# Layer 1 of a two-layer kernel: row maxima turned by DMA, projection tiles in the score banks, value pieces in halves

## What is computed

```python
Xn = (X - mu) * rsqrt(var + LN_EPS) * ln_w + ln_b
Q, K, V = split(einsum('bsd,df->bsf', Xn, W_in), 3)      # 16 heads of 16 channels
Q, K = _rope(Q), _rope(K)
scores = einsum('bhqd,bhkd->bhqk', Q, K) / sqrt(16)       # 1024 x 1024, no mask
ctx = einsum('bhqk,bhkd->bhqd', softmax(scores), V)
out = einsum('bsd,df->bsf', ctx, W_out) + X
```

## Time and profile before

| | us |
|---|---|
| median of 3 runs | 1045.62 (1043.57 to 1057.51) |
| the profiled execution | 1048.43 |
| its span, first to last instruction | 1046.6 |
| busy: PE, DVE, POOL, ACT | 924.7, 855.2, 705.1, 684.8 |

### The profile page before, as it was taken

How to read it: one execution, slowest core, us unless ns; L and a number is a source line. 1 busy time by engine, 2 the same in 40 slices (tenths; PEclk the granted TensorE clock), 3 DMA queues, 4 the chain that set the end, 5 groups by cost and what they waited for, 6 DMA issues and landing times. The chain is left out here.

```text
span 1046.6 us, 26415 instructions
## 1 busy us (share of the span) xinstructions
PE 924.7 (88%) x8703; PEld 514.1 (49%) x8703; DVE 855.2 (82%) x1760; ACT 684.8 (65%) x1779; POOL 705.1 (67%) x1034
## 2 busy tenths in 40 slices
PE   3588898998998998998998987788999999999998
PEld 2365665765666666665665665433222222323223
DVE  6797868788888888888788786578999999999871
ACT  2555655655655656565665554217999999898895
POOL 4668878788788888888888878342766765544231
PEclk9698989999999999999999998879999999999999
DMA  5655653454444543444554444243221122222101
GB/s 194 127 115 122 105 95 75 93 106 80 93 97 83 95 99 80 91 98 81 94 98 78 90 86 90 52 131 62 63 38 26 23 42 42 52 40 49 28 1 42
DMA packets 247995, 82.57 MB, mean 79 GB/s; under 512 B 222196, under 2 KB 246452, under 8 KB 247604
## 3 DMA queue, kind: packets, MB, share of 16 engines
q1 hardware_dynamic: 247428, 78.53, 37.5%
q10 hardware_dynamic: 432, 2.36, 0.6%
HBM read 18.49 MB, written 4.19 MB: 22 GB/s over the span
## 5 line engine op out<-in xcount | busy, mean ns | idle before, releaser
L1343 DVE TENSOR_REDUCE l_mxv<-l_mx 128x1 f32<-128x1024 f32 x256 | 294.9, 1214 | 26.2 <-PE l_mx L1545 25.4
L1256 ACT ACTIVATE l_prob<-l_sc 128x512 f32<-128x512 f32 x512 | 273.3, 604 | 17.6 <-PE l_sc L1553 16.5
L427 ACT ACTIVATE an<-an 128x256 f16<-128x256 f32 x128 | 53.3, 416 | 212.8 <-DVE an L601 212.8
L752 POOL TENSOR_TENSOR t<-t 128x320 f32<-128x320 f32 x128 | 110.6, 864 | 114.0 <-DVE t L648 113.9
L1545 PE MATMUL l_mx<-early 48*128 48x512 f16 x512 | 156.3, 387 | 17.7 <-DVE l_mxv L1343 14.5
L743 POOL TENSOR_TENSOR rm<-ss,half_neg 128x5 f32<-128x5 f32 x128 | 156.5, 1223 | 0.0
L1553 PE MATMUL l_sc<-early 50*128 50x512 f16 x512 | 155.7, 382 | 0.3 <-ACT l_prob L1256 0.3
L1516 PE MATMUL l_acc<-l_prob,qkv_all 128*17 128x256 f32 x2048 | 153.9, 384 | 0.0
L881 PE MATMUL qk<-early,xh 128*128 128x384 f16 x512 | 131.2, 339 | 4.4 <-issue 4.0
L934 PE MATMUL ob<-wo_hi,ats 128*128 128x256 f16 x512 | 108.4, 279 | 28.2 <-DMA ats<-an 22.7
L868 PE MATMUL pv<-v,probs 128*64 128x65 f32 x2048 | 90.4, 232 | 29.3 <-ACT probs L476 22.2
(11 more groups left out here) (191 smaller groups left out, 2069.6 us busy)
## 6 DMA issues: line engine op xcount, KB each, us to landing
qkv_all<-w_qkv SPq DMA_DIRECT2D x3, 768.0 KB, 8.5
v<-v SPq DMA_DIRECT2D x64, 32.5 KB, 2.0
xn_all<-xs SPq DMA_DIRECT2D x16, 128.5 KB, 2.1
xa<-x SPq DMA_DIRECT2D x16, 128.0 KB, 2.5
tk<-nat SPq DMA_TRANSPOSE x128, 2.8
qkv_all<-w_o SPq DMA_DIRECT2D x8, 256.0 KB, 3.9
ats<-an SPq DMA_TRANSPOSE x128, 2.5
xc<-x SPq DMA_DIRECT2D x16, 128.0 KB, 2.3
```

Source lines behind the costliest of these rows:

```text
L427: return act.activation(dst, src, ACT.Copy, scale=scale)
L752: pool.tensor_tensor(t1[:, b, :, :], t1[:, b, :, :], t2[:, :, :], ALU.add).then_inc(s_["pool_u"], 1)
L1256: act.activation(prob[:, (y * NI + u) % NPR, h * 512:(h + 1) * 512], sc[:, k % NSC, :], ACT.Exp, scale=D1 ** -0.5).then_inc(s_["act_sc"], 1)
L1343: dve.tensor_reduce(mxv[:, x % 2, u:u + 1], mx[:, MX[k] % 2, :], AX.X, ALU.max).then_inc(s_["dve_mx"], 1)
```

## The change

It touches layer 1 alone, in three parts. **Maxima:** `mhl` is now padded to 128 columns, and SP turns it with a DMA transpose straight into `mrow`, waits for that and issues the two row DMAs. PE's transpose, ACT's copy and the unit M are gone. **Projection tiles:** Y and Z are now units Y of the ring `sc`, in eighth 2 of slots 25 to 36 (and four places in slots 37 and 38), in two parts: `rows(i, 0)` behind the pair of half 0, `rows(i, 1)` with the routed matmuls behind the pair of half 1. DVE's add stands ahead of the reduce of that eighth. **Value pieces:** `PIECE_AT` has two places for each piece; part 0 is groups 0 and 1, part 1 groups 2 and 3. `READ` and `MADE` replace the plain numbers in the waits, as DVE now reads some units of `sc`; `free(k)` is the wait for a bank. Of the rest of the diff, POOL's `mhl` writes `mhl[:, b, 0:NI]` and `mhl[:, b, NI:2 * NI]` and waits for `max_turned`.

```diff
-AHEAD_AT = ((33, 3), (34, 3), (35, 3), (36, 3), (37, 2), (37, 5), (38, 1), (38, 4))
+AHEAD_AT = ((33, 2), (34, 2), (35, 2), (36, 2), (37, 2), (37, 5), (38, 1), (38, 4))
+ROW_AT = 2
...
-PIECE_AT = (7, 9, 9, 11, 13, 15, 17, 19)
+PIECE_AT = ((6, 7), (8, 9), (10, 10), (11, 12), (13, 14), (15, 16), (17, 17), (18, 19))
...
-    for k, place in enumerate(PIECE_AT):
-        back, r = divmod(place, 2 * NI)
-        if r == 2 * u + h and 0 <= y - back < ITEMS:
-            yield y - back, k
+    for k, places in enumerate(PIECE_AT):
+        for part, place in enumerate(places):
+            back, r = divmod(place, 2 * NI)
+            if r == 2 * u + h and 0 <= y - back < ITEMS:
+                yield y - back, k, part
...
-def ahead(c, u):
-
-    return AHEAD_AT.index((c, u)) if (c, u) in AHEAD_AT else None
+def rows_at(c, u):
+
+    if (c, u) in AHEAD_AT:
+        return NI + AHEAD_AT.index((c, u))
+    return c - SLOT_Y if u == ROW_AT and 0 <= c - SLOT_Y < NI else None
...
-                order += [("E", c - LAG_E, u, h) for h in range(2)]
-            if u == 4 and 0 <= c - LAG_M < ITEMS:
-                order.append(("M", c - LAG_M))
+                order.append(("E", c - LAG_E, u, 0))
+            if rows_at(c, u) is not None:
+                order.append(("Y", rows_at(c, u)))
+            if 0 <= c - LAG_E < ITEMS:
+                order.append(("E", c - LAG_E, u, 1))
             if fold_at(c, u) is not None:
                 order.append(("F", fold_at(c, u)))
...
-            if u == 3 and 0 <= c - SLOT_Y < NI:
-                order.append(("Y", c - SLOT_Y))
-            if ahead(c, u) is not None:
-                order.append(("Z", ahead(c, u)))
...
-    SC = score_units()
+    order = score_units()
+    SC = {unit: k for k, unit in enumerate(order)}
+    READ = {unit: sum(o[0] != "Y" for o in order[:k + 1]) for unit, k in SC.items()}
+    MADE = {unit: k + 1 + (unit[0] == "Y") - (order[k - 1][0] == "Y") for unit, k in SC.items()}
...
-        mhl = sb("mhl", [P, 2, 2, NI], F16)
-        mrow = sb("mrow", [2 * NI, 2, P], F16)
+        mhl = sb("mhl", [P, 2, P], F16)
+        mrow = sb("mrow", [P, 2, P], F16)
...
                 r = t + LAG_M - SLOT_Y - 1
+                sp.wait_ge(s_["pool_mh"], t + 1)
+                if t >= 2:
+                    sp.wait_ge(mr_st[t % 2], t // 2 * 32)
+                sp.dma_start_transpose(mrow[:, t % 2, :], mhl[:, t % 2, :]).then_inc(s_["max_turned"], 16)
+                sp.wait_ge(s_["max_turned"], 16 * (t + 1))
+                for j in range(2):
+                    sp.dma_start(qt[row + j:row + j + 1, tile % 4, :],
+                                 mrow[j * NI:(j + 1) * NI, t % 2, :]).then_inc(mr_st[t % 2], 16)
                 if 0 <= r < NI:
                     n = TILES[r]
-                    sp.wait_ge(s_["dve_mx"], MX["Y", r] + 1)
+                    sp.wait_ge(s_["dve_sc"], r + 1)
                     sp.dma_start(out[n * P:(n + 1) * P, :], ysb[:, r % 4, :]).then_inc(y_st[r % 4], 16)
-                sp.wait_ge(s_["act_sc"], SC["M", t] + 1)
-                for r in range(2):
-                    sp.dma_start(qt[row + r:row + r + 1, tile % 4, :],
-                                 mrow[r * NI:(r + 1) * NI, t % 2, :]).then_inc(mr_st[t % 2][r], 16)
...
-                    t = c - LAG_M
-                    if u == 4 and item(t):
-                        k = SC["M", t]
-                        act.wait_ge(s_["pe_sc"], k + 1)
-                        for r in range(2):
-                            wait(act, mr_st[t % 2][r], t // 2 * 16)
-                        ev(mrow[:, t % 2, :], sch[k % NSC][0:2 * NI, 0:P]).then_inc(s_["act_sc"], 1)
...
+                    i = rows_at(c, u)
+                    if i is not None:
+
+                        k = SC["Y", i]
+                        dve.wait_ge(s_["pe_sc"], MADE["Y", i])
+                        dve.wait_ge(s_["pool_base"], i + 1)
+                        if 4 <= i < NI:
+                            dve.wait_ge(y_st[i % 4], 16 * (i // 4))
+                        dst = ysb[:, i % 4, :] if i < NI else x1s[:, TILES[i], :]
+                        dve.tensor_tensor(dst, sc[:, k % NSC, 0:D], x1s[:, TILES[i], :], ALU.add
+                                          ).then_inc(s_["dve_sc"], 1)
...
+            def free(k):
+
+                if k >= NSC and order[k - NSC][0] == "Y":
+                    pe.wait_ge(s_["dve_sc"], order[k - NSC][1] + 1)
+                elif k >= NSC:
+                    pe.wait_ge(s_["act_sc"], READ[order[k - NSC]])
+
+            def piece(v, k, part):
+
+                if k == part == 0:
                     if v == 0:
                         pe.wait_ge(s_["set_acc"], 1)
                     wait(pe, s_["act_acc"], v)
-                pe.wait_ge(s_["act_sc"], SC["E", v, k, 1] + 1)
-                for g in range(4):
+                pe.wait_ge(s_["act_sc"], READ["E", v, k, 1])
+                for g in range(part * 2, part * 2 + 2):
                     ins = pe.matmul(acc[g * CGR:g * CGR + VW, 0:D], vv1[:, v // H1, k, v % H1, :],
                                     prob[:, (v * NI + k) % NPR, g * D:(g + 1) * D], start=(k == 0), stop=(k == NI - 1))
-                ins.then_inc(s_["pe_pv"], 1)
+                if part == 1:
+                    ins.then_inc(s_["pe_pv"], 1)
+
+            def rows(i, part):
+
+                k = SC["Y", i]
+                dst = sc[:, k % NSC, 0:D]
+                if part == 0:
+                    if i == 0:
+                        pe.wait_ge(s_["mod_dve"], MOD["blks"])
+                        pe.wait_ge(s_["pool_wo"], 2)
+                    if i < NI:
+                        pe.wait_ge(c0_ld[i // 4], 16 * 2)
+                    elif i == NI:
+                        pe.wait_ge(c1_ld, 16 * 2)
+                    free(k)
+                for n, (l, w) in enumerate(((0, wou_hi), (0, wou_lo), (1, wou_hi))):
+                    if i < NI:
+                        pe.matmul(dst, ctt0[:, i, l, part, :], w[:, part, :], start=(part == 0 and n == 0), stop=False)
+                    elif part == 0:
+                        pe.matmul(dst, ctt1[:, i - NI, l, :], w[:, 0, :], start=(n == 0), stop=False)
+                if part == 1:
+                    routed(dst, i // NI, i % NI).then_inc(s_["pe_sc"], 1)
...
-                        for v, k in pieces_at(y, u, h):
-                            piece(v, k)
-
-                    t = c - LAG_M
-                    if u == 4 and item(t):
-
-                        k = SC["M", t]
-                        pe.wait_ge(s_["pool_mh"], t + 1)
-                        if t == 0:
-                            pe.wait_ge(s_["mod_act"], MOD["hid1s"])
-                        wait(pe, s_["act_sc"], k + 1 - NSC)
-                        pe.transpose(sch[k % NSC][0:2 * NI, 0:P], mhl[:, t % 2, :, :].rearrange("p r i -> p (r i)"),
-                                     idh[:, :]).then_inc(s_["pe_sc"], 1)
```

More of the change, by code:

```diff
@@ L1151, in layer1 @@
         turned = [[loads[a * 2 + j] for j in range(2)] for a in range(2)]
-        mr_st = [[sem(f"max_placed{r}_{j}") for r in range(2)] for j in range(2)]
+        mr_st = [sem(f"max_placed{j}") for j in range(2)]
         y_st = [sem(f"y_stored{j}") for j in range(4)]
@@ L1172, in turn @@
                 if tile >= 4:
-                    sp.wait_ge(s_["pe_sc"], SC["E", last_of(tile - 4), NI - 1, 1] + 1)
+                    sp.wait_ge(s_["pe_sc"], MADE["E", last_of(tile - 4), NI - 1, 1])
                 for a, dst in enumerate((qt, kt)):
@@ L1385, in _ @@
             pool.memset(less1[:, :, :], -1.0).then_inc(s_["set_pool1"], 1)
-            pool.wait_ge(s_["set_pool1"], 1)
+            pool.memset(mhl[:, :, :], 0.0).then_inc(s_["set_pool1"], 1)
+            pool.wait_ge(s_["set_pool1"], 2)
             def normalised(t):
                 b = t % 2
-                pool.wait_ge(s_["act_sc"], SC["F", t] + 1)
+                pool.wait_ge(s_["act_sc"], READ["F", t])
                 pool.tensor_tensor(rcs[:, b, :, :], ctf[:, b, :, :, D1], less1[:, :, :], ALU.pow
@@ L1537, in _ @@
                     if item(y) and u == 0:
-                        for r in range(2):
-                            pe.wait_ge(mr_st[y % 2][r], 16 * (y // 2 + 1))
+                        pe.wait_ge(mr_st[y % 2], 32 * (y // 2 + 1))
                     for h in range(2):
@@ L1551, in _ @@
                             r, k = HB * half, SC["E", y, u, h]
[L1552 removed]
+                            free(k)
                             pe.matmul(sc[:, k % NSC, :], kt[r:r + KS + 2, tile % 4, u * P:(u + 1) * P],
                                       qt[r:r + KS + 2, tile % 4, keys], start=True, stop=True).then_inc(s_["pe_sc"], 1)
[L1556 to L1568 removed]
+                        if rows_at(c, u) is not None:
+                            rows(rows_at(c, u), h)
+                        for v, k, part in pieces_at(y, u, h):
+                            piece(v, k, part)
                     t = fold_at(c, u)
@@ L1577, in _ @@
```

(23 more changed lines are left out.)

38 lines of the change are left out of this document (9 added, 29 removed).

## The result

The changed kernel takes **1161.4 us** (median, 1158.47 to 1171.91, 4 runs), the kernel before 1046.97 beside it; the ratio is 1.107, 95% interval 1.100 to 1.115: slower by 11%. The forecast was 1160. The profiled execution has a span of 1161.0, so 114.4 more than before. The granted clock is 0.88 in the first slot with values and 1.00 in all slots after it.

What follows compares the result with a forecast made beforehand. Before: PE, DVE and ACT all at 96%, no single bound. 62.0 + 28.5 + 13.0 + 8.2 + 2.5 = 114.2 on 1048.43 gave 1162.6, less 2.8 for the median: 1160 us, range 1135 to 1182.

Steps and rivals of the forecast that it cites:

- The main term: Value pieces on PE: a half piece costs what a whole one does, so 14 blocks instead of 7, +4.05 us a slot.
- the stall: PE's wait for a bank in eighth 2 of a plain slot: 0.51 before, 0.36 after, so -0.15 us a slot.
- The transpose's -0.15: The maxima's transpose on PE, 749.36 to 749.51, falls away: -0.15 us a slot.
- 17 plain slots: Layer 1's slots without projection tiles: 13.2 us each, together +62.0.
- The tile slots: Slots that also project: eight at 14.2 us, +28.5, and four with shorter tiles at 13.9, +13.0.
- Ends: Last two slots, 14.4 us against 10.31 each, +8.2; first slot with values, 12.1 plus up to 1.5 of waits, +2.5.
- Ahead of the values: Before 713.95 us, where the change does not reach: everything stays, nothing added.
- The total: Sum of all terms over the profiled execution: +114.2 us.
- Maxima by DMA: SP's queue: row copies land 8.9 us after a slot's begin, needed at 13.2, so hidden with 4 us.
- (A): Rival: two column groups stream in half the time, halves smooth PE's supply to DVE, 1027 us; chance 0.04.
- (B): Rival: passes cost, but their change in and out hides under the pairs, plain slot 11.8, 1118 us; chance 0.05.
- (C): Rival: SP's chain is the bound, with a small transpose of 7.5 or more, 1230 us; chance 0.04 with other unseen waits.

Runs made afterwards that it cites:

- experiment 4: Changed kernel with each of the twelve half pieces of a head issuing all four column groups instead of two: 1174.13 us, ratio 1.125 to the kernel before.
- experiment 1: Kernel before with only the value pieces in halves at the change's places; maxima on PE and tiles in the maxima's ring stay: 1173.12 us, ratio 1.120.
- experiment 2: Changed kernel with value pieces whole again at the old places; maxima by DMA and tiles in the score ring stay: ratio 1.0018 to the kernel before.
- experiment 3: Kernel before with the maxima turned by DMA and nothing else, pieces and tiles as before: ratio 0.999 to the kernel before.
- experiment 6: Whole pieces, one in each eighth, first in the changed kernel (1040.42 us, ratio 0.993), then in the kernel before with transposes on PE (ratio 0.993).
- experiment 7: Changed kernel with whole pieces one in each eighth and DVE's add moved behind the reduce: 1045.57 us, ratio 0.997 to the kernel before.
- experiment 8: Kernel before with maxima by DMA and whole pieces one in each eighth, tiles in the maxima's ring: 1040.98 us, ratio 0.990.

## Why the prediction was right, step by step

**The main term.** "A half piece costs what a whole one costs" was read from matmuls in ones, twos and fours that all gave 0.22 a pass. The changed kernel has 0.86 against 0.88, experiment 4 shows that the other two groups are nearly free, and experiment 1 that this part alone gives the whole loss. The slot rose by 3.83 from 9.52; with the stall shorter by 0.11 and the transpose worth 0 to 0.03, the main term comes out at 3.94 to 3.97, where +4.05 was forecast.

**The transpose's -0.15 was mis-sized.** It is 0.03 between whole pieces (experiments 2 and 3) and nothing between halves (experiment 1). I took the distance of two starts, 749.36 to 749.51, for the price of what stood there. Without it the block needs 0.12 longer to the fold, as experiment 2's 0.99 shows. The stall was 0.40 instead of 0.36. These two, 0.16 to 0.19, were partly covered by the main term, 0.1 too high. The sum itself, 9.52 + 4.05 - 0.15 - 0.15, is 13.27; written as 13.2 it lost another 0.07. So the slot has 13.35 for 13.2, and 17 plain slots came to +64.5 and not +62.0.

**The tile slots** came to 14.33 and 13.79 for 14.2 and 13.9; together +42.2 against +41.5. Against their own plain slots the full tiles cost 0.98, where 1.0 was forecast. What I didn't see is what experiment 2 showed: with whole pieces, the same move costs 0.3. In the changed kernel PE was so slow that DVE's wait for the tile hid under it.

**Ends.** The first slot with values was to be 13.1 and is 14.25. The forecast held the clock at 1.00, and it was granted at 0.88 in this slot; 12% of 14.25 is 1.7, an estimate of what that can cost, and enough for the miss of 1.15. The last two and the tail gave +7.5 for +8.2.

**Ahead of the values** the forecast put nothing, and the profile of after is 3.5 shorter (710.46 against 713.95). Of that, 2.0 lie ahead of layer 1's slots (681.14 against 683.12), in work that the change doesn't touch; this time goes from 676.46 to 683.12 in the eleven profiles. The other 1.5 lie in slots 5 and 6: 14.83 and 14.49 for 16.10 and 14.73, with a clock of 0.65 for 0.59 in slot 5 and of 1.00 in slot 6 in both. About the same lengths come back in experiment 6, 16.15 and 14.73 with the transposes on PE and 14.86 and 14.49 with the maxima by DMA, so they may belong to that part of the change; no run tests it.

**The total is right in part by luck.** The plain slots missed by +2.5, the tiles by +0.7, the first slot by +1.2, the tail by -0.7 and the stretch ahead by -3.5: together +0.2. The mechanism and the main term hold without that; that 114.2 stood for 114.4 doesn't.

**Maxima by DMA** were hidden, as forecast. The small transpose lands in 2.3, below the 2.7 and 3.2 between which it was put. Experiment 6 shows that the chain even holds a slot of 9.34: row copies are never waited for there. What the forecast didn't see is that they were the less safe before. With the transpose on PE, SP issued them 6.3 after a slot's begin, by DMA 4.0 to 4.7 (753.12 in a slot begun at 749.10, experiment 6). Every profile in which PE waits for them has the transposes on PE: once in the kernel before, for 0.26, and three times in experiment 6. A second long slot of the kernel before, 9.72, has no releaser in the trace.

**The rivals.** (A), two groups in half the time, fell with experiment 4. (B), the change in and out hidden, fell with the 0.86. (C), SP's chain as the bound, is out in every kernel run with the maxima by DMA. The idea behind (A), that evenness between PE and DVE would pay, holds in part: it is reached with whole pieces, and brings a plain slot of 9.34, not 9.15.

## What to carry to other kernels

In this kernel matmuls side by side in column groups cost one pass together, so the unit to move about is the full set: splitting it and setting the halves apart doubled its cost, while pairing halves of different sets was free. When engines are within a few per cent of each other, first give each eighth the same work; that brought 0.7%, and 1.0% with the maxima by DMA, which alone, in an uneven slot, brought nothing that a measurement could tell (0.1%). And the distance between two starts isn't what a small instruction costs if its neighbours would need that time to change over.

## What the runs showed of the hardware that I had not expected

- A column group that a neighbour leaves free is filled by a matmul of another kind: the 16-column transpose of the maxima ran beside half a piece, starts 0.01 apart (experiment 1).
- The same work ran at two clocks in the two slots of the router and dense layers (columns as above), in the changed kernel:

```profile
681.14:710.46 29.32, 27.29 (x127) 13.31 (x128) 22.18 (x28) 7.02 (x15) 9.67 (x26) 0.83 0.50 136
```

and in that of experiment 3:

```profile
676.54:694.69 18.15, 16.41 (x55) 5.48 (x56) 11.85 (x20) 1.87 (x3) 7.08 (x17) 0.53 0.67 188
694.69:717.85 23.16, 22.89 (x73) 13.47 (x73) 10.52 (x9) 5.14 (x12) 2.54 (x9) 0.56 0.10 25
```

A granted clock of 0.53 to 0.56 is near the lower of the two levels (1.2 of 2.4 GHz), and these slots took 12 us more. Five of the eleven profiles show it, with 41 to 44 us in these slots (experiments 1, 2, 3, 7 and 8), and six, with 29 to 32, do not. What decides it stays open; no run tests it.
